# A decoder of six layers: a written-out round with a slot for every piece in the first and last phase, and the first phase's residual sums on VectorE

## The reference, cut to what matters

```
x = x + rotary_attention(layernorm(x))           # 16 heads, causal; q, k are sines and cosines out of a table
x = x + cross_attention(layernorm(x), ctx)       # 16 heads, softmax, scores clipped; biases
x = x + experts(layernorm(x))                    # 16 experts, top 1, capacity
x = x + tanh_attention(layernorm(x))             # one head
x = x + cross_attention(layernorm(x), ctx)       # 16 heads, softmax
x = x + feed_forward_fp4(layernorm(x))           # inputs and hidden values rounded to FP4; silu(gate) * up, down
```

## Time and profile before

| | |
|---|---|
| median of 3 runs | 3547.66 us (3538.26 to 3547.86) |
| the profiled execution | 3541.41 us, its span 3539.7 us |
| mean granted TensorE clock | 0.973 |
| TensorE busy | 3196.1 us, 90% of the span |
| VectorE busy | 2292.2 us, 65% |
| ScalarE busy | 1832.0 us, 52% |
| GpSimd busy | 1276.2 us, 36% |
| the first phase | up to about 1490 us |
| the last phase | from about 2180 us |

### The profile page before, as it was taken

The page is one execution under the profiler, slowest core; times in us unless marked ns, Lnnn a source line. Parts: engine busy times, 40 slices in busy tenths (PEclk is TensorE's granted clock), DMA queues, the critical chain, the costliest instruction groups (busy, mean ns, idle before and its releaser), DMA issues. The chain is left out here.

```text
span 3539.7 us, 58174 instructions
## 1 busy us (share of the span) xinstructions
PE 3196.1 (90%) x21558; PEld 2184.7 (62%) x21558; DVE 2292.2 (65%) x4717; ACT 1832.0 (52%) x3307; POOL 1276.2 (36%) x1933
## 2 busy tenths in 40 slices
PE   4899999999999998699999786899999999999996
PEld 2566666666666665366666453566666666666664
DVE  3577777777777776332111583777777777777774
ACT  3777777888777775211111232444555454554442
POOL 3455555556555554100000450223233333232322
PEclk9999999999999999799999897999999999999998
DMA  4977777767777774333333344334433344433330
GB/s 97 158 102 99 102 102 102 105 96 95 101 103 98 102 93 60 110 115 112 112 111 105 100 151 75 47 53 64 67 53 54 53 61 64 62 53 54 54 46 12
DMA packets 291102, 301.19 MB, mean 85 GB/s; under 512 B 35242, under 2 KB 278426, under 8 KB 290820
## 3 DMA queue, kind: packets, MB, share of 16 engines
q1 hardware_dynamic: 276420, 273.41, 47.9%
q0 software_dynamic: 6144, 15.68, 1.5%
q10 hardware_dynamic: 8256, 8.39, 0.7%
HBM read 95.51 MB, written 50.40 MB: 41 GB/s over the span
## 5 line engine op out<-in xcount | busy, mean ns | idle before, releaser
L504 DVE TENSOR_REDUCE xa_mx<-bank 128x2 f32<-128x512 f32 x1024 | 652.8, 686 | 211.5 <-PE bank L494 209.2
L608 ACT ACTIVATE xa_p<-bank 128x512 f32<-128x512 f32 x1024 | 571.0, 597 | 360.3 <-PE bank L598 358.5
L619 DVE SCALAR_TENSOR_TENSOR xa_p<-xa_p,bank 128x1024 f32<-128x1024 f32 x256 | 306.6, 1216 | 13.5 <-ACT xa_p L608 6.8
L935 ACT ACTIVATE xa_p<-bank 128x384 f32<-128x384 f32 x512 | 238.1, 493 | 85.8 <-PE bank L923 63.9
L631 PE MATMUL bank<-xa_p,xa_v 128*32 128x256 f32 x4096 | 277.5, 389 | 2.1 <-DVE xa_p L619 2.1
L598 PE MATMUL bank<-ex_w,xa_ks 99*128 99x256 bf16 x1024 | 192.1, 280 | 71.7 <-ACT xa_p L608 37.4
L1959 POOL DMA_INDIRECT sa_y<-expert_out,sa_s x64 | 69.8, 1091 | 512.0 <-POOLq L1860 484.6
L1754 ACT ACTIVATE ex_h<-bank,ex_b 128x512 f32<-128x512 f32 x64 | 44.0, 687 | 361.8 <-PE bank L1743 361.8
L1743 PE MATMUL bank<-ex_xt,ex_w 128*128 128x512 f32 x512 | 224.6, 597 | 0.7 <-ACT ex_xt L1734 0.7
L1773 PE MATMUL bank<-ex_w,ex_h 128*128 128x256 f32 x1024 | 224.0, 379 | 1.0 <-issue 0.9
L1558 POOL TENSOR_TENSOR fp_v<-fp_v,fp_p 128x1408 f32<-128x1408 f32 x32 | 101.5, 3171 | 313.1 <-DVE fp_v L1549 313.1
(11 more groups left out here) (290 smaller groups left out, 6800.7 us busy)
## 6 DMA issues: line engine op xcount, KB each, us to landing
ex_w<-ra_parts SPq DMA_DIRECT2D x384, 128.0 KB, 5.9
xa_ks<-xa_pk SPq DMA_DIRECT2D x384, 128.0 KB, 4.4
ex_w<-in_L_ffn_W SPq DMA_DIRECT2D x32, 1024.0 KB, 7.2
xa_qs<-xa_pq SPq DMA_DIRECT2D x192, 128.0 KB, 7.0
ex_w<-xa_pq SPq DMA_DIRECT2D x192, 128.0 KB, 6.6
ra_x<-in_x SPq DMA_DIRECT2D x32, 256.0 KB, 9.9
xa_ctx<-in_ctx_t SPq DMA_DIRECT2D x64, 128.0 KB, 4.7
queue<-zeros ACTq DMA_DIRECT2D x4, 2048.0 KB, 7.8
```

Of the source, the lines that this page charges most:

```text
L504: c.nc.vector.tensor_reduce(c.xa.row_max[:, :, n], halves(c.banks[2 + n % 2]), AX.X, ALU.max).then_inc(s.max_taken, 1)
L608: c.nc.scalar.activation(c.xa.p_beside[:, n // 2 % 4, :, n % 2, :], halves(c.banks[n % 2]), ACT.Exp, scale=SCALE).then_inc(s.exp, 1)
L619: c.nc.vector.scalar_tensor_tensor(out=p, in0=p, scalar=1.0, in1=c.banks[bank][:, :].unsqueeze(1).broadcast_to([P, TC, 2 * S]), op0=ALU.mi ...
L935: c.nc.scalar.activation(c.xa.p_after[:, n // 2 % 4, n % 2, 0:S + P], c.banks[n % 2][:, 0:S + P], ACT.Exp, scale=1.0 / math.sqrt(2.0 * DH) ...
```

## The change

`due` takes a list of slots, one for each k, instead of first, gap and count. Each engine has a round of its own, whose length is the number of its pieces for one item (82, 41, 52, 29 and 8 in the first phase; 58, 31, 34, 7 and 6 in the last), so that every slot of a round holds exactly one piece. `token_residual` goes; both projections of the first phase are plain `token_matmuls`, and the residual is added on VectorE as PSUM is emptied (`dve_ra_add`, `dve_a_end`). `dve_a_end` has the wait for the biased x1 that `pe_a_project` had. The computation stays the same.

```diff
-def due(n, period, first, gap=1, count=1):
-
-    for b in range(max(0, -(-(n - first - gap * (count - 1)) // period)), min(B - 1, (n - first) // period) + 1):
-        k, off = divmod(n - first - b * period, gap)
-        if off == 0:
+def due(n, period, slots, items=B):
+
+    for k, slot in enumerate(slots):
+        b, off = divmod(n - slot, period)
+        if off == 0 and 0 <= b < items:
             yield b, k
...
-def token_residual(c, bank, left, right, residual):
-
-    ps = c.banks[bank]
-    for tc in range(TC):
-        out = ps[:, tc * D:(tc + 1) * D]
-        c.nc.tensor.matmul(out, c.consts.ident[:, :], residual[:, tc, :], start=True, stop=False)
-        for k in range(KC):
-            m = c.nc.tensor.matmul(out, left[:, k, tc * P:(tc + 1) * P], right[:, k, :], start=False, stop=(k == KC - 1))
-    return m
...
-    token_residual(c, bank, c.ra.o_t, c.wa.Wo, c.ra.x[b % 4]).then_inc(s.projected, 1)
+    token_matmuls(c, bank, c.ra.o_t, c.wa.Wo).then_inc(s.projected, 1)
     c.bank_out[bank] = (s.added, b + 1)
 
 
-def act_ra_add(c, bank, b):
+def dve_ra_add(c, bank, b):
 
     s = c.ra.s
-    c.act.wait_ge(s.projected, b + 1)
-    c.act.wait_ge(s.ended, b - 3)
-    c.nc.scalar.activation(c.ra.x1[b % 4][:, :, :], halves(c.banks[bank]), ACT.Copy).then_inc(s.added, 1)
+    c.dve.wait_ge(s.projected, b + 1)
+    c.dve.wait_ge(s.ended, b - 3)
+    c.nc.vector.tensor_tensor(c.ra.x1[b % 4][:, :, :], halves(c.banks[bank]), c.ra.x[b % 4][:, :, :], ALU.add).then_inc(s.added, 1)
...
-    c.pe.wait_ge(c.ra.s.x1, b + 1)
-    c.pe.wait_ge(*c.bank_out[bank])
-    token_residual(c, bank, c.xa.o_t, c.wx.Wo, c.ra.x1[b % 4]).then_inc(s.projected, 1)
+    c.pe.wait_ge(*c.bank_out[bank])
+    token_matmuls(c, bank, c.xa.o_t, c.wx.Wo).then_inc(s.projected, 1)
     c.bank_out[bank] = (c.ra.s.ended, b + 1)
 
 
-def act_a_end(c, bank, b):
+def dve_a_end(c, bank, b):
 
     s, r, par = c.ra.s, c.ra, b % 2
-    c.act.wait_ge(c.xa.s.projected, b + 1)
-    c.act.wait_ge(s.x2_out[par], 16 * (b // 2))
-    c.act.wait_ge(c.rt.s.xn, b - 1)
-    c.nc.scalar.activation(r.x2[par][:, :, :], halves(c.banks[bank]), ACT.Copy).then_inc(s.ended, 1)
+    c.dve.wait_ge(c.xa.s.projected, b + 1)
+    c.dve.wait_ge(s.x1, b + 1)
+    c.dve.wait_ge(s.x2_out[par], 16 * (b // 2))
+    c.dve.wait_ge(c.rt.s.xn, b - 1)
+    c.nc.vector.tensor_tensor(r.x2[par][:, :, :], halves(c.banks[bank]), r.x1[b % 4][:, :, :], ALU.add).then_inc(s.ended, 1)
...
-SLOTS_A = 84
-LAST_A = (B - 1) * SLOTS_A + 894
+ROUND_A = dict(pe=82, dve=41, act=52, pool=29, sp=8)
 
 
 def pe_phase_a(c):
-    for n in range(LAST_A):
-        for b, k in due(n, SLOTS_A, 797, 8, 4):
+    period = ROUND_A["pe"]
+    for n in range((B - 1) * period + 981):
+        for b, _ in due(n, period, (567,)):
+            pe_ra_turn(c, b)
+        for b, _ in due(n, period, (581,)):
+            pe_ra_values(c, b)
+        for b, k in due(n, period, (671, 672, 677, 679, 682, 683, 685, 688, 689, 694, 695, 698, 699, 701, 703, 705)):
+            pe_ra_score(c, b, k)
...
+        for b, k in due(n, period, (691, 696, 706, 708)):
+            pe_ra_sum(c, b, k)
...
 def dve_phase_a(c):
-    for n in range(LAST_A):
-        for b, _ in due(n, SLOTS_A, 602):
+    period = ROUND_A["dve"]
+    for n in range((B - 1) * period + 498):
+        for b, _ in due(n, period, (236,)):
+            dve_ra_stats(c, b)
...
+        for b, _ in due(n, period, (368,)):
+            dve_ra_add(c, 6, b)
...
+        for b, _ in due(n, period, (483,)):
+            dve_a_end(c, 6, b)
...
-        for b, _ in due(n, SLOTS_A, 625):
-            act_ra_add(c, 6, b)
-        for b, _ in due(n, SLOTS_A, 865):
-            act_a_end(c, 6, b)
...
+        for b, _ in due(n, period, (223,)):
+            pool_ra_low(c, b, 0)
+        for b, _ in due(n, period, (225,)):
+            pool_ra_low(c, b, 1)
+        for b, k in due(n, period, (231, 232, 234, 235, 236, 237, 238, 239, 240, 242, 243, 244, 245, 246, 247, 249)):
             pool_ra_mask(c, b, k)
...
-SLOTS_E = 80
-LAST_E = (B - 1) * SLOTS_E + 580
+ROUND_E = dict(pe=58, dve=31, act=34, pool=7, sp=6)
 
 
 def pe_phase_e(c):
-    for n in range(LAST_E):
-        for b, k in due(n, SLOTS_E, 221, 9, 4):
+    period = ROUND_E["pe"]
+    for n in range((B - 1) * period + 1100):
+        for b, _ in due(n, period, (818,)):
+            pe_xa_keys(c, 7, c.wx, B + b)
+        for b, _ in due(n, period, (846,)):
+            pe_xa_values(c, 7, c.wx, B + b)
...
+        for b, k in due(n, period, (881, 884, 888, 891, 893, 895, 896, 898, 900, 901, 903, 905, 907, 909, 911, 913)):
+            pe_xa_max(c, B + b, k)
```

401 lines of the change are left out of this document (195 added, 206 removed).

## The result

| | median | runs | ratio to before (95%) |
|---|---|---|---|
| before | 3547.76 us | 4 | |
| after | 3379.32 us (3377.41 to 3381.31) | 4 | 0.9531 (0.9513 to 0.9549) |

The change takes 168 us off; 107 were forecast. The profiled execution has a span of 3375.9 us for 3539.7: 163.8 us less. Three marks divide it. Up to the first matmul of the experts it needs 1408.9 us for 1491.0, so the first phase gave 82 us; the two phases between gave 2; from the first keys matmul of the last phase to the end are 1311.0 us for 1390.9, 80 us. The forecast had 80 for the first and 27 for the last.

The account below looks back on a forecast made before the run. The prediction took TensorE, busy 95% in both phases, to set the pace. It summed 80 us (first phase) and 27 us (last) to 107 off the profiled 3541.4, giving 3434 and a predicted median of 3441 us, range 3395 to 3500.

Parts of the forecast that it names:

- the term of the last phase: Last phase, same work in a new order: 27 intervals by 1.0 = 27 us off, bounds 0 and 68 us.
- the walk: One round of all engines followed head by head with traced durations: first phase 39.0 us, last phase 39.5.
- The rest of the round: Last phase, the round apart from the stretch from score 1 to score 15: 28.1 us, against 27.8 before.
- The first phase's two terms: First phase: 28 intervals by 2.6 are 73 us, the other four by the matmuls alone 7; together 80 us.
- TensorE sets the pace, so I count them in full: First phase: the removed residual matmuls count fully, 1.73 us an item, times 32 = 55 us.
- nothing, if another engine sets it afterwards: First phase: lower bound of the gain from the removed residual matmuls, against 55 us in full.
- the price put on the residual matmuls: First phase: the four pairs of identity matmuls of an item cost TensorE 8 x 0.216 = 1.73 us.
- VectorE's queue in front of ra_values: First phase, VectorE's pieces from projection to ra_values: 8.3 us against TensorE's 8.6, so the sum is covered with 0.3 spare.
- the slower rival: ra_stack DMAs land late and ra_score 0 waits; gain eaten at 12.4 us, 3569 at 13; chance 0.09.
- Only the matmuls pay: Rival: the removed matmuls give 55 us, the order nothing; 3492, with some disorder 3475 to 3510; chance 0.18.
- VectorE sets the pace: Rival, first phase: VectorE's queue exceeds the spare 0.3 us, as by GpSimd collisions; 54 us lost, 3495; chance 0.08.
- Better than walked: Rival: all fits better, rounds of 38.0 and 38.7 us; 165 us off, 3383; chance 0.05.

Follow-up runs that it names:

- e18: Kernel after, with gates 2 and 3 of the last phase behind maximum 15 on TensorE: 3427.81 us, 0.9678.
- e10: Kernel after, with e_down ahead of e_up 3 on TensorE, and e_normed and e_out ahead of hidden 3 on VectorE: 3463.35 us, 0.9775.
- e1: Kernel before, with the residual sums on VectorE alone, at the old places: 3554.04 us, 1.0033.
- e2: Changed kernel with the old last phase, so the change in the first phase alone: 3454.83 us, 0.9750.
- e4: Kernel after, with the residuals added on TensorE and the copies on ScalarE as before; order otherwise new: 3424.10 us, 0.9667.
- e12: Kernel after, with one more VectorE pass over bank 6 directly ahead of ra_add in the first phase: 3394.01 us, 0.9576.
- e7: e1 with GpSimd's and SP's new round in the first phase: 3536.27 us, 0.9981.
- e11: e7 with rt_counts behind xa_sum 1 on TensorE: 3543.67 us, 1.0000.
- e5: Kernel before, with e_down behind e_up 3 on TensorE and e_out behind hidden 3 on VectorE: 3753.4 us, 1.0595.
- e6: Kernel after, with the last phase's maxima 0 to 7 back among scores 8 to 15 on TensorE: 3559.95 us, 1.0044.
- e9: e5 with e_normed on VectorE moved between hidden 3 and e_out: 3571.0 us, 1.0074.
- e13: e7 with ra_turn behind score 9 on TensorE: 3523.23 us, 0.9944.
- e17: e7 with the sum and xa_stats ahead of rt_choose on VectorE: 3492.37 us, 0.9850.

## Why the prediction was wrong

**What failed: the term of the last phase.** "27 by 1.0 = 27 us" measured 80. Two things are in it: the steady round was priced too long, and what fills and drains the phase was put at nothing, without a reason.
- The steady round was mis-sized: 38.56 us where the walk said 39.5 and the sum took 39.6, so 2.05 us an item instead of 1.0, 28 us in all. From score 1 to 15 the walk had 11.4, the trace has 11.17. "The rest of the round" was to be 28.1, slower than the 27.8 before, and is 27.39: most of the miss. At which piece the walk lost these 0.7 us isn't on record. The trace shows that TensorE's matmuls wait for nothing in that stretch, although short maxima stand in it. What covers them is seen in e18 (1.6 us for two gates) and e10 (1.8 us for the swap). Together they are more than 2.05; the order before had covers of its own there, so neither is a share of the gain.
- Filling and draining were not counted at all: 24.4 us. In the fill before, TensorE waited 5.4 us once for hidden 3, 11.4 for the stack's DMAs and 6.0 for that of the rows; after, 0.7, 9.6 and 3.6. Its granted clock in the two intervals of 35.59 and 43.27 us was 0.95 and 0.88, and 1.00 and 0.95 in those of 32.49 and 37.35. In the drain before it waited 7.3 and 14.6 us for the last two items to be quantised, after 0.7 and 14.7, and 2.5 for an input. No run takes these 24.4 us apart further.

With the first phase's 82 us (70.4 + 11.7) where 80 (73 + 7) were taken, and 2 from the phases between, the 57 us between sum and measurement are complete. The first phase's two terms were off by 3 and 5 us, in opposite directions.

**"TensorE sets the pace, so I count them in full."** The amount came out, the reason given doesn't hold. In the old order the matmuls are worth nothing (e1, +9 us): one residual's time is lost again to VectorE's queue ahead of rt_counts, the other's to GpSimd ahead of the keys. The lower bound "nothing, if another engine sets it afterwards" is what happens, and it isn't an engine with more work, but two whose queues stand in an unlucky order. By runs that each add one thing, up to e2's 90 us: sums on VectorE +9, GpSimd and SP -18, sum ahead of choose -44, the order of TensorE, ScalarE and the rest of VectorE -37; between runs of different chips a step is good to some 4 us. In rounds at full clock: 41.85, 41.7, 41.2, 40.2, 39.3 us. The first three steps, 1.7 us, come near the price put on the residual matmuls (1.73), and the last, 0.9 us, near what the walk gave to order; that these sizes agree is no proof that they are the same things. Another sequence splits it otherwise: by e4 order alone gives 1.2 and the sums then 1.3. That 80 came so near 82 is in part luck: two errors cancel, and the argument for the matmuls was wrong. The walk did use the new order of VectorE's queue, in which the sum is covered.

**What held.** L503 is 39.30 us apart (39.2). The sum takes 0.685 us (0.69), VectorE is busy for 86% (85), L464 is gone. VectorE's queue in front of ra_values has little room: TensorE waits 0.24 us there at 709.81, and 0.2 are to spare (e12) where 0.3 was said. The Trainium skill (Perfetto Trace Analysis, Optimizing Scalar/DVE Operations) puts the access overhead on PSUM higher for VectorE than for ScalarE, which speaks against the move. This case agrees on the direction: ScalarE's copy L1013 took 0.597 us, the sum takes 0.685. But it was the place in the queue that decided the sign. ra_stack's DMAs land in 6.6 us in the median and 10.4 at worst, under the 12.4 of the slower rival, and L912 waited for one only once, 7.9 us in the fill.

**The rivals.** "Only the matmuls pay" is false: they alone pay nothing. "VectorE sets the pace" was given for a collision with GpSimd; the largest L293 is 1.23 us in the new kernel, the median 0.41, and there is no such loss. But its mechanism, a queue on VectorE that is late, is what TensorE waits for in e1, e7 and e11. "Better than walked", 3383, has almost the measured time, by wrong parts: rounds of 38.0 and 38.7 where 39.30 and 38.56 were measured. Its first phase is 31 us too good, its last 29 us too bad for want of filling and draining.

**Open.** How TensorE's and ScalarE's new orders share the last 37 us of the first phase; whether statistics ahead of choose would have paid without the sums; how the 2.05 us of the last phase divide between its places; and what in the new order shortens fill and drain. The queues fit only together, and a single move (e5, e6, e9) tests the mixture as much as the move.

## What to carry to other kernels

When work leaves the busiest engine, look for an idle gap of another engine ahead of the first instruction that depends on it: VectorE stood idle for 1.2 us with a ready sum behind a waiting rt_choose, and putting it first was worth over 40 us while the removed matmuls without it were worth nothing. When an instruction can wait for several others, look at the end of each of them, not only at the one that the profile names. Count what a change of order does in the fill and the drain too, where every wait is exposed; here that was 36 of 164 us. A round written out by hand is one object over all its queues: moving one matmul group and the instruction that empties its bank cost 209 us (e5).

## What the runs showed of the hardware

TensorE's granted clock fell to half behind short idle gaps, in some rounds and not in others of the same order. e10, stretches of 2 us in one round (columns as in the earlier trace rows):

```profile
2667.47:2669.47 2.00, 1.21 (x8) 0.54 (x8) 1.93 (x3) 1.35 (x3) 0.18 (x1) 1.00 0.00 0
2669.47:2671.47 2.00, 1.80 (x18) 0.71 (x18) 1.90 (x4) 1.41 (x3) 0.00 (x0) 0.67 0.00 0
2671.47:2673.47 2.00, 2.00 (x14) 1.15 (x7) 1.93 (x3) 0.78 (x2) 0.00 (x0) 0.50 0.04 8
2673.47:2675.47 2.00, 2.00 (x12) 1.50 (x10) 1.97 (x2) 0.41 (x2) 0.00 (x0) 0.97 0.00 0
```

The clock is 0.50, the lower of its two levels (1.2 GHz), for some 3.5 us, and the round takes 41.9 us instead of 40.35. Ahead of it TensorE had a gap of 0.74 us at 2660.45 and then gaps of 0.62, 0.47 and 0.20 us; the next round has the same gaps, a clock of 1.00 throughout and no loss. Ten rounds of e10, ten of e1 (1.4 us each), five of e7 and nearly all of e5 and e6 have it; e13, e17 and the kernel after, in their steady rounds, don't. So a wait of about a microsecond can cost more than itself: at 1.6 us for each such round, 16 of e10's 84 us, and in e1 14 us, more than the whole loss of 9. Which rounds are hit, these runs don't show.
